# Turning the keys of an attention stage on VectorE instead of TensorE, with other DMA shapes

## The reference, cut to what matters

```python
# conditioning: one stage id per sequence, one bias per token
bias = braak_embed[braak_stages][..., None]
q = query + bias                                    # query = x
attn = softmax(einsum('bsd,btd->bst', q, key))      # key = value = side
t_in = einsum('bst,btd->bsd', attn, value)
# feed-forward: RMS norm, gate with the top 2 of 8 experts, SwiGLU with low-rank parts
nx = t_in * rsqrt(mean(t_in * t_in) + EPS) * norm_w
...
out = x + sum over experts of weight * out_e
```

## Time and profile before

| | |
|---|---|
| median of 3 runs | 1298.62 us (1297.87 to 1300.12) |
| the profiled execution | 1297.99 us, of which the span is 1296.2 us |
| PE busy in the span | 1290.6 us |
| DVE, ACT, POOL busy in the span | 857.3, 531.0, 232.2 us |
| the chain that ended last | 99% PE |
| granted TensorE clock | 1.0 of full speed throughout |

### The profile page before, as it was taken

How to read it: one execution, slowest core, us unless ns; L and a number is a source line. 1 busy time by engine, 2 the same in 40 slices (tenths; PEclk the granted TensorE clock), 3 DMA queues, 4 the chain that set the end, 5 groups by cost and what they waited for, 6 DMA issues and landing times.

```text
span 1296.2 us, 18613 instructions
## 1 busy us (share of the span) xinstructions
PE 1290.6 (100%) x7190; PEld 1128.8 (87%) x7190; DVE 857.3 (66%) x1582; ACT 531.0 (41%) x991; POOL 232.2 (18%) x189
## 2 busy tenths in 40 slices
PE   9999999999999999999999999999999999999998
PEld 8999988888888888888888888888888888888887
DVE  6898756656665666656665766566665776575656
ACT  6877744324333334333433333333433333333332
POOL 3444530202020200202020202020110202020200
PEclk9999999999999999999999999999999999999999
DMA  9777730010202020102011020202020101102000
GB/s 287 160 170 170 178 97 1 30 46 1 74 2 73 1 73 2 60 15 48 26 31 45 1 74 2 73 1 74 2 62 12 54 21 39 37 3 71 1 17 17
DMA packets 116419, 69.73 MB, mean 54 GB/s; under 512 B 57694, under 2 KB 107372, under 8 KB 116204
## 3 DMA queue, kind: packets, MB, share of 16 engines
q1 hardware_dynamic: 116020, 68.54, 19.2%
q10 hardware_dynamic: 312, 0.02, 0.0%
HBM read 51.40 MB, written 17.14 MB: 53 GB/s over the span
## 4 chain that ended last, share of the span: by engine, by line
PE 99%; ACT 0%; DVE 0%; issue 0%; DVEq 0%
PE bank L1295 31%; PE bank L1294 31%; PE bank L1296 31%; PE bank L1421 2%; PE bank L1347 1%; PE bank L1399 1%; PE bank L1340 1%; PE bank L1306 0%; ACT prob L739 0%; PE bank L1386 0%; DVE x_out L1238 0%; ACT qT_hi L722 0%; PE bank L1314 0%; PE bank L1429 0%; PE bank L1428 0%; PE bank L1364 0%
## 5 line engine op out<-in xcount | busy, mean ns | idle before, releaser
L1166 DVE TENSOR_TENSOR act_a<-silu_a,bank 128x512 f32<-128x512 f32 x128 | 87.7, 685 | 211.6 <-PE bank L1296 195.0
L830 ACT ACTIVATE br_hi<-act_br 128x512 fp32r<-128x512 f32 x128 | 80.9, 632 | 188.0 <-DVE act_br L1177 188.0
L823 ACT ACTIVATE silu_b<-bank 128x512 f32<-128x512 f32 x128 | 76.2, 595 | 187.9 <-PE bank L1296 187.1
L1295 PE MATMUL bank<-w2T_lo,s_hi 128*128 128x256 f32 x512 | 144.7, 283 | 0.0
L1296 PE MATMUL bank<-w2T_hi,s_lo 128*128 128x256 f32 x512 | 143.3, 280 | 0.0
L1294 PE MATMUL bank<-w2T_hi,s_hi 128*128 128x256 f32 x512 | 142.7, 279 | 0.0
L1174 DVE TENSOR_TENSOR act_b<-silu_b,bank 128x512 f32<-128x512 f32 x128 | 88.0, 687 | 80.9 <-PE bank L1296 80.0
L660 POOL TENSOR_TENSOR t_lo<-t_in,t_hi 128x512 fp32r<-128x512 f32 x32 | 40.6, 1290 | 552.5 <-ACT t_hi L810 552.3
L819 ACT ACTIVATE silu_a<-bank 128x512 f32<-128x512 f32 x128 | 75.7, 591 | 134.8 <-PE bank L1296 134.7
L679 POOL TENSOR_TENSOR v_lo<-v_full,v_hi 128x512 fp32r<-128x512 f32 x64 | 94.6, 1510 | 136.6 <-ACT v_hi L815 136.6
L1187 DVE TENSOR_TENSOR br_lo<-act_br,br_hi 128x512 fp32r<-128x512 f32 x128 | 104.8, 819 | 5.6 <-ACT br_hi L830 3.1
(11 more groups left out here) (201 smaller groups left out, 3215.6 us busy)
## 6 DMA issues: line engine op xcount, KB each, us to landing
kv<-in_fside_BxSxS SPq DMA_DIRECT2D x32, 256.0 KB, 3.1
t_scratch<-oT SPq DMA_DIRECT2D x32, 256.0 KB, 2.5
t_in<-t_scratch SPq DMA_DIRECT2D x32, 256.0 KB
out<-x_out SPq DMA_DIRECT2D x52, 128.0 KB
x_in<-in_x SPq DMA_DIRECT2D x96, 64.0 KB, 2.7
x_out<-in_x SPq DMA_DIRECT2D x48, 128.0 KB
rho<-scale_scratch SPq DMA_DIRECT2D x16, 256.0 KB
rstd<-scale_scratch SPq DMA_DIRECT2D x16, 256.0 KB
```

Source lines behind the costliest of these rows:

```text
L823: nc.scalar.activation(silu_b[:, :], h1_bank[j % 2][:, :], ACT.Silu).then_inc(silu_b_ready, 1)
L830: nc.scalar.activation(br_hi[j % 2][:, :], act_br[j % 2][:, :], ACT.Copy).then_inc(br_hi_ready, 1)
L1166: nc.vector.tensor_tensor(act_a[j % 2][:, :], silu_a[j % 2][:, :], h3_bank[j % 2][:, :], ALU.mult).then_inc(act_a_ready, 1)
L1295: nc.tensor.matmul(dst, w_hi, x_lo, start=False, stop=False, skip_group_check=not grouped)
```

## The change

It makes `TURNED` reach to the last sequence, and has VectorE turn the keys as well. A second copy of `side` is loaded in block order (`k_pair`), next to the natural one (`kv`) that the values need. DVE turns it straight into PSUM (`turn_k`, into `kT_bank`), ACT and DVE take the high and low parts from there through a strided view. PE's transpositions of keys (sequences 6 to 31) and queries (30 and 31) are gone. The low part of the turned q moves from DVE to POOL (`turned_q_low`). Since q and k are now turned alike, the order of the features is free: the runs are 64 numbers, tokens stay in natural order, one transfer covers two sequences of one group of 64 features (`load_x_pair`, `load_k_pair`, four transfers each), and the second stage loads and stores in plain order with fewer transfers. The load of `bias_rep` becomes four transfers and stands behind three weight loads.

```diff
-TURNED = range(6, BATCH - 2)
+TURNED = range(6, BATCH)
...
+            def load_x_pair(c):
+                if c - RING in TURNED:
+                    sp.wait_ge(q_turned, turned_no(c - RING + 1))
+                else:
+                    sp.wait_ge(q_ready, c - RING + 2)
+                for g in range(P // BLK):
+                    rows = x_pair[pair_at(c)][g * BLK:(g + 1) * BLK].rearrange("p k h d -> p (k h d)")
+                    sp.dma_start(rows.rearrange("p (n y) -> p n y", n=2 * BLOCKS),
+                                 x_blocks[g][:, BLOCKS * c:BLOCKS * (c + 2)]).then_inc(x_pair_loaded[pair_at(c)], 16)
+
+            def load_k_pair(c):
+                if c - RING in TURNED:
+                    sp.wait_ge(k_turned, turned_no(c - RING + 1))
...
             def step(c):
+                if c % 2 == 0 and c + 4 in TURNED:
+                    load_x_pair(c + 4)
+                if c % 2 == 1 and c + 3 in TURNED:
+                    load_k_pair(c + 3)
                 if 5 <= c + 3 < BATCH:
                     load_kv(c + 3)
-                if c + 4 < BATCH:
+                if c + 4 < BATCH and c + 4 not in TURNED:
                     load_xs(c + 4)
                 store(c - 1)
...
+            def turned_q_low(c):
+                pool.wait_ge(qT_hi_ready, c + 1)
+                hi, lo = qT[c % 2]
+                nc.gpsimd.tensor_tensor(in_blocks(lo[:, :]), blocks_of(q[c % 2][:, :, :]), f32(in_blocks(hi[:, :])),
+                                        ALU.subtract).then_inc(qT_lo_ready, 1)
...
             def step(c):
                 if DVE_BIAS <= c + 2 < BATCH:
                     add_bias(c + 2)
+                if c + 1 in TURNED:
+                    turned_q_low(c + 1)
                 value_low(c)
...
+            def turn_k(c):
+                dve.wait_ge(k_pair_loaded[pair_at(c)], pair_count(c))
+                dve.wait_ge(kT_hi_ready, c)
+                dve.wait_ge(kT_lo_ready, c)
+                nc.vector.transpose(kT_bank[:, :], k_in[c % RING][:, :]).then_inc(k_turned, 1)
...
                 if c + 1 < BATCH:
-                    qk_low(c + 1)
+                    if c + 1 not in TURNED:
+                        q_low(c + 1)
+                    k_low(c + 1)
...
                 if c + 2 in TURNED:
                     turn_q(c + 2)
+                    turn_k(c + 2)
                 probT_low(c)
...
                 if c + 1 < BATCH:
-                    transpose_qk(c + 1)
+                    if c + 1 not in TURNED:
+                        transpose_q(c + 1)
+                        transpose_k(c + 1)
```

More of the change, by code:

```diff
@@ L153, in adaln_moe_ffn @@
         bias_rep = sb(early, "bias_rep", [P, BLOCKS, BATCH])
[L154 to L157, removed]
+        opening = ExitStack()
+        embed_in = sb(opening, "embed_in", [STAGES, S])
+        itok_in = sb(opening, "itok_in", [STAGES, BATCH], I32)
+        itok_f = sb(opening, "itok_f", [STAGES, BATCH])
+        stage_hot = sb(opening, "stage_hot", [STAGES, BATCH])
+        opening.close()
+        k_pair = [sb(early, f"k_pair{k}", [P, 2, DC * S]) for k in range(RING // 2)]
+        k_in = [k_pair[k // 2][:, k % 2] for k in range(RING)]
         early.close()
@@ L362, in xs_count, with pair_at, pair_count, plain_no @@
         def xs_count(c):
-            return 16 * sum(P // BLK if k in TURNED else 1 for k in range(c % RING, c + 1, RING))
+            return 16 * (c // RING + 1)
+        def pair_at(c):
+            return c // 2 % (RING // 2)
+        def pair_count(c):
+            return 16 * P // BLK * sum(2 * m in TURNED for m in range(pair_at(c), c // 2 + 1, RING // 2))
         def turned_no(c):
             return c - TURNED[0] + 1
-        def mixed(c):
-            return c * TILE // S in TURNED
+        def plain_no(c):
+            return sum(k not in TURNED for k in range(c + 1))
         def as_blocks(ap):
@@ L444, in load_kv @@
                              ).then_inc(kv_loaded[c % RING], 16)
+            def load_x_pair(c):
[10 more added lines that the diff above has]
+                    sp.wait_ge(k_turned, turned_no(c - RING + 1))
+                for g in range(P // BLK):
+                    rows = k_pair[pair_at(c)][g * BLK:(g + 1) * BLK].rearrange("p k n -> p (k n)")
+                    sp.dma_start(rows.rearrange("p (n y) -> p n y", n=2 * BLOCKS),
+                                 side_blocks[g][:, BLOCKS * c:BLOCKS * (c + 2)]).then_inc(k_pair_loaded[pair_at(c)], 16)
             def store(c):
@@ L494, in _ @@
                              ).then_inc(b2_loaded, 16)
+            sp.wait_ge(bias_stored, 16)
+            for g in range(P // BLK):
+                sp.dma_start(bias_rep[g * BLK:(g + 1) * BLK], bias_scratch.rearrange("(j s) b -> s j b", s=BLK)
+                             ).then_inc(bias_rep_loaded, 16)
             for c in range(1, ROWS_STEP):
@@ L1411, in attend, with gate_half, wait_gate @@
                 last.then_inc(o_ready, 1)
-            def gate(c, first=False):
+            def gate_half(c, h):
+                for dc in range(DC):
+                    last = nc.tensor.matmul(gate_bank[:, h * GATE_STRIDE:(h + 1) * GATE_STRIDE],
+                                            oT[c % 2][:, dc, h, 0:P], oT[c % 2][:, dc, h, 0:GATE.stop],
+                                            start=(dc == 0), stop=(dc == DC - 1))
+                if h == SC - 1:
+                    last.then_inc(gate_ready, 1)
+            def wait_gate(c, first=False):
                 if first:
@@ L1418, in gate @@
                 pe.wait_ge(oT_copied, c + 1)
+            def gate(c, first=False):
+                wait_gate(c, first)
                 for h in range(SC):
-                    for dc in range(DC):
-                        last = nc.tensor.matmul(gate_bank[:, h * GATE_STRIDE:(h + 1) * GATE_STRIDE],
-                                                oT[c % 2][:, dc, h, 0:P], oT[c % 2][:, dc, h, 0:GATE.stop],
-                                                start=(dc == 0), stop=(dc == DC - 1))
-                last.then_inc(gate_ready, 1)
+                    gate_half(c, h)
             def transpose_rows(r, dst):
```

118 lines of the change are left out of this document (58 added, 60 removed).

## The result

The changed kernel takes **1303.09 us** (median of 17 runs, 1299.93 to 1305.63), the kernel before 1298.39 (17 runs, 1296.76 to 1300.12). The ratio is 1.0035, with a 95% interval of 1.0027 to 1.0042: slower by about a third of a per cent. Forecast were 1297.0 and a range to 1302, so the time lies outside, on the slow side.

A forecast was written before the change was run, and what follows sets the result against it. PE was taken to bound the kernel, with DVE second by some tenths. The terms -12.3 + 7.0 + 1.0 + 2.4 + 0.3 gave -1.6 us, so 1296.4 profiled and 1297.0 as median; range 1290 to 1302 (8 in 10).

The forecast's parts named there:

- SP and the load of k: Near step 26: SP's queue brings k(28) 5.6 us late, 3.2 tolerated, costing +2.4 us once; bounds 0 to 4.
- a DMA bound over all 24 steps: Rival, chance 0.17: 1024 KB a step fills the DMA engines, the 24 steps become 5.0 us, 1303 to 1309 in all.
- the cheap end: Case where a DMA packet costs the same whatever its size: share 0.89 at 4.21 us a step, hidden.
- The 0.44 off each free step: PE loses 28 groups of four transpositions, 12.3 us in all; plain steps go from 4.65 to 4.21 us.
- The turn into PSUM: DVE's turn of k written to PSUM: 0.62 us start to start, with 1.4 as upper bound.
- DVE held by POOL: Steps 11 to 20: small routing pieces on DVE wait for POOL's third instruction; ten steps take 49.4 us, +7.0 net.
- 5.7 + 1.1: Step 11: 5.7 us with its routing piece blocked by POOL, plus 1.1 as its last piece runs into value_lo.
- the two scalings of t: Steps 28 and 29: DVE instructions with two SBUF inputs, the first held by 1.0 us; +1.0 in all.
- The +0.3 for the early loads: Steps 1 to 3: kv and bias_rep moved behind other transfers, estimated to cost +0.3 us.
- the slow side: Outcome slower than the kernel before, given 0.17: DMA becomes the bound, 1303 to 1309 us.

The follow-up runs named there:

- run 6: Changed kernel, but from sequence 10 on each key-pair transfer brings only the first sequence of the pair (wrong scores); 1299.05 us, ratio 1.0008 to the kernel before.
- run 5: Changed kernel with the stores of results to the scratch tensor issued from ScalarE's queue instead of SyncE's; 1297.17 us, ratio 0.9992 to the kernel before.
- run 2: Changed kernel with key pairs loaded only for sequences 6 to 9, stale keys turned from 10 on; 1295.36 us, ratio 0.9969 to the kernel before.
- run 7: Changed kernel with the keys of sequences 26 to 31 transposed by TensorE again, their pairs not loaded; 1297.64 us, ratio 0.9992 to the kernel before.
- run 9: Changed kernel with key pairs from sequence 10 on read as contiguous 4 KB rows (wrong layout), same bytes and transfers; 1300.00 us, ratio 1.0008.
- run 1: Changed kernel with POOL's low part of the turned queries cut to the first of eight column blocks; 1296.24 us, ratio 0.9986 to the kernel before.
- run 3: Changed kernel with POOL's low part of the turned queries waiting until VectorE's routing piece is through; 1298.60 us, ratio 0.9994 to the kernel before.
- run 12: Changed kernel with POOL's low part replaced by a one-input product with zero, leaving the low part out; 1296.75 us, one run.
- run 8: Changed kernel with POOL's low part after the routing piece, the last six sequences' keys on TensorE, and kv(5) loaded earlier; 1292.15 us, ratio 0.9951.

## Why the prediction was wrong

**The step that failed is "SP and the load of k".** It was put at +2.4 us once near step 26, bounded by 4, and measured 38.65 less 29.1 to 29.4, that is 9.2 to 9.6. Four things in it were off.
- *The landing,* the largest. I took 2.7 us from issue to landing, a median of a kernel that moved fewer bytes. Here it was 5.45 for k(26) and 6.16 for k(28), at shares of 1.00 and 0.82 while they were under way; in run 6, with half of the keys, 3.63 and 4.23. With 2.7 at the same issue times k(26) would have been in time and k(28) late by 1.6 in place of 5.07.
- *The issue.* I took SP's lengths from before, 18.9 us from the store of step 21 to k(28). It was 20.4 (121.87 to 142.30), as kv held SP for 2.3 to 2.6 at a time: 1.5 us more.
- *The pair ahead.* I had one late pair. The pair after it, k(30), was on time, as I said; but k(26) ahead of it was late too, by 2.16 in step 24, and a pair of x held POOL for 2.4 in step 26.
- *The clock,* which fell behind the long wait; step 27 took 6.44 where run 6 has 3.90.

The two waits for k, 7.2 us, and these 2.5 come to 9.7, about the whole of the 9.2 to 9.6.

**The price was in the prediction, in the wrong place.** I weighed a DMA bound over all 24 steps as a rival at 0.17, to decide at a 256-byte packet that costs twice a 128-byte one, and dismissed the cheap end as hidden. In the traces a 128-byte packet takes 13 ns and a 256-byte packet 18, 1.4 times as much: 184 / 0.81 = 227 GB/s for full engines before, 212 / 0.83 = 255 after. That carries 1024 KB in 4.1 us, so plain steps did reach 4.2, and the rival as I drew it (steps of 5.0) did not come. But 4.1 of 4.2 leaves nothing for 1.31 MB more. The sum that I left out is one line: bytes of steps 21 to 27 over the rate. It gives 7 x 4.1 + 5.1 = 33.8 us, 4.4 more than 29.4: a warning, though only half of the loss, and no floor, as run 5 passed the stretch in 31.56. Runs 2, 6, 7 and 9, which each took load away and gained, show that this stretch is bound by transfers; run 5 shows that SP's order adds to it. How the loss divides between the two can't be read from these runs, as each mends part of the other.

**The clock, which the prediction had at full.** A fall to half came after step 11 and after the long wait for k. Step 12 took 5.41 in the changed kernel and 4.46 in run 2, where the clock stayed at 1.00 after the same idle time of PE; windows of run 2:

```profile
70.00:75.00 5.00, 3.18 (x28) 2.97 (x27) 4.83 (x13) 2.78 (x8) 3.24 (x3) 1.00 0.39 116
75.00:79.00 4.00, 4.00 (x35) 3.78 (x34) 3.90 (x13) 3.43 (x9) 2.04 (x2) 1.00 0.65 150
```

Run 5 had this fall too (step 12 at 5.41); runs 6, 7 and 9 did not, with the same 6.64 to 6.65 us for step 11. So a stall of PE may or may not be followed by a fall; the one after step 11 costs 1.0 us in step 12 and 0.6 over the ten steps (49.69 against 49.05). It fits the wider spread of the changed kernel's runs (5.7 us against 3.4), but that link is argued, not shown.

**What was right.** The 0.44 off each free step (4.19 to 4.22). The turn into PSUM, 0.59 start to start against 0.62. DVE held by POOL: 49.69 against 49.4, or 49.05 without the fallen clock, which the prediction did not have, so that part of the agreement is luck. (Its single steps add up to 49.3.) Runs 1 and 3 show that it is POOL's instruction. Step 11 took 6.64 where I had 5.7 + 1.1, with both of its pieces held to the end; at a full clock (run 6) steps 12 to 20 are within 0.25 of what I drew, 13, 15, 17 and 20 at 5.15, 5.19, 4.97 and 5.19. The Trainium skill, SBUF — State Buffer (Who interferes with whom), says that copy and tensor_scalar on VectorE can enter a mode in which they contend with GpSimd, and that instructions with two SBUF inputs contend with a GpSimd instruction that reads SBUF. g_logits, with one input, at 1.14 agrees with the first; my prediction had counted instructions with one SBUF input as free. The same section of the Trainium skill has the later one blocked until the other is through; run 12 shows 0.49 where that would be 1.32, and 0.17 for g_z with its two inputs, not held at all, so there the measurement differs. Of the two scalings of t the second was held, 1.64 in step 29, not the first as I had it; together they came to 9.35 against 9.5. The +0.3 for the early loads was too little: step 4 alone was longer by 0.6, and with kv(5) issued earlier, in run 8, by 0.1.

**The rivals.** The range ended at 1302 because the slow side hung on one mechanism that the plain steps would refute. A local form of it, in the five steps where other loads come, is what the runs showed, and it had no line.

## What to carry to other kernels

When a change shortens a loop and adds bytes to it, divide the bytes of each stretch by the rate at a full DMA share, and do it again for the stretch in which other transfers come; a latency from a lighter load does not hold under a heavier one (2.7 us before, 5.45 and 6.16 here). When work is moved to POOL, look at what VectorE runs in those 1.3 us: it was a wait on POOL, not less work, that took 4.8 us off the ten steps here. And a change that is slower as a whole may hold a gain: with three edits around it, POOL's low part behind the routing piece, the stores from ACT's queue and kv(5) issued earlier, this one is 0.65% faster than the kernel before.

## What the runs showed of the hardware

- A POOL instruction with one input (1.50 us) delayed a small tensor_scalar on VectorE by 0.3 and a small two-input instruction beside it not at all (0.17); POOL instructions with two inputs (1.28 and 1.26) held a tensor_scalar and a two-input instruction to their ends (1.14 and 1.25).
- Issuing the same 256 KB store from ScalarE's queue in place of SyncE's raised the DMA rate over 50 us from 217 to 242 GB/s (share 0.86 to 0.94).
- Packets of 128 bytes took 13 ns and packets of 256 bytes 18 ns on the DMA engines, so the longer ones carry a byte for 0.7 of the price.
- A transposition on TensorE that reads every second 4-byte column took 0.65 for four, 0.05 us more than one of neighbouring columns, and VectorE's turn with the same stride took 0.70, as without.
